# Shorter steps for the edge loop of a graph layer: 3 tiles and 32 nodes a step, the fold in four column groups

## What is computed

```
msg  = relu(x_norm[src] + edge_attr @ W_e + b_e)        # 21250 x 512
aggr = segment_sum(msg, dst, num_segments=1250)         # 1250 x 512
h    = (1 + eps) * x_norm + aggr
h    = silu(bn(h @ W1 + b1)) ; h = silu(bn(h @ W2 + b2)) ; x = x + h
x    = x + experts(layernorm(x))
```

## Time and profile before

| | |
|---|---|
| median of 3 executions | 615.01 us (614.53 to 616.93) |
| the profiled execution | 615.38 us, of which the span of the trace is 613.6 us |
| PE busy in the span | 492.7 us (80%) |
| DVE, ACT, POOL busy | 391.9, 324.5, 257.3 us |
| mean granted clock of PE | 0.91 |
| edge loop, from the first gather to the first matmul behind the loop | 30.4 to 283.9 us |
| relu of a tile (L611) | 596 ns, 167 times |

### The profile page before, as it was taken

One profiled execution on the slowest core, in us unless ns is written; L12 is line 12 of the kernel. 1 busy time (PEld: TensorE's weight loads), 2 busy tenths in 40 slices (PEclk: granted clock), 3 DMA queues, 4 the chain that ended last, 5 costly groups with the idle time before them and its releaser, 6 DMA issues.

```text
span 613.6 us, 11694 instructions
## 1 busy us (share of the span) xinstructions
PE 492.7 (80%) x4023; PEld 317.0 (52%) x4023; DVE 391.9 (64%) x961; ACT 324.5 (53%) x660; POOL 257.3 (42%) x245
## 2 busy tenths in 40 slices
PE   2469769899899989998999965702599999999990
PEld 2313223333333333343466434502599999999980
DVE  5847767667666666664689457685766767665530
ACT  3526555455555555544684057534066667566650
POOL 1077777777777777100000000000535564655341
PEclk9959899899999999998999987855599999999996
DMA  9887777777777777217079007910159999974331
GB/s 220 256 300 241 213 209 230 227 221 228 228 216 230 227 225 230 64 44 266 22 262 285 20 14 222 313 62 1 51 188 290 271 301 282 278 206 75 48 44 21
DMA packets 48944, 112.46 MB, mean 183 GB/s; under 512 B 7144, under 2 KB 7564, under 8 KB 48885
## 3 DMA queue, kind: packets, MB, share of 16 engines
q0 software_dynamic: 18992, 54.02, 32.3%
q1 hardware_dynamic: 29399, 57.16, 29.2%
q10 hardware_dynamic: 494, 0.52, 0.4%
HBM read 98.88 MB, written 12.79 MB: 182 GB/s over the span
## 4 chain that ended last, share of the span: by engine, by line
PE 63%; DVE 11%; ACT 9%; DMA 5%; issue 5%; POOL 2%; DVEq 1%; SPq 1%; POOLq 0%; ACTq 0%
PE bank L1355 22%; PE bank L1536 11%; PE bank L1325 11%; PE bank L1346 7%; ACT big L611 3%; DVE bank L977 3%; PE bank L1562 2%; PE bank L1334 2%; PE bank L1526 2%; PE bank L1517 2%; POOL pair L486 1%; DVE rows_z L1176 1%; PE bank L1399 1%; PE bank L1405 1%; DMA xs_home<-in_x 1%
## 5 line engine op out<-in xcount | busy, mean ns | idle before, releaser
L1325 PE MATMUL bank<-big,edge_home 128*64 128x256 f32 x668 | 109.4, 420 | 30.9 <-ACT big L611 30.5
L611 ACT ACTIVATE big<-bank 128x512 f32<-128x512 f32 x167 | 99.5, 596 | 65.1 <-DVE bank L977 63.5
L496 POOL DMA_INDIRECT big<-token_rows,idx x32 | 37.4, 1170 | 222.4 <-DVE idx L1234 215.0
L486 POOL DMA_INDIRECT pair<-node_rows,edge_home x97 | 96.3, 993 | 29.6 <-issue 28.7
L1355 PE MATMUL bank<-big,pair 128*128 128x156 f16 (+2 forms) x1056 | 106.5, 260 | 1.1 <-DVE big L1033 0.9
L1355 PEld LDWEIGHTS bank<-big,pair 128*128 128x128 f16 x1056 | 80.9, 97 | 24.6 <-issue 1.4
L486 POOL DMA_INDIRECT big<-node_rows,edge_home x70 | 70.5, 1006 | 49.3 <-issue 48.3
L1325 PEld LDWEIGHTS bank<-big,edge_home 128*64 128x64 f32 x668 | 35.4, 140 | 88.3 <-issue 58.4
L1346 PE MATMUL bank<-edge_home 64*128 64x512 f16 x501 | 73.6, 401 | 3.9 <-DVE edge_home L950 3.9
L505 POOL DMA_INDIRECT out<-rows_z,idx x32 | 51.5, 1610 | 43.8 <-issue 24.6
L977 DVE TENSOR_TENSOR bank<-pair,bank 128x512 f32<-128x512 f32 x97 | 64.1, 687 | 6.2 <-PE bank L1346 6.1
(11 more groups left out here) (222 smaller groups left out, 778.0 us busy)
## 6 DMA issues: line engine op xcount, KB each, us to landing
raw<-in_L_ffn_w SPq DMA_DIRECT2D x12, 1024.0 KB, 8.3
edge_home<-in_L_ffn_w SPq DMA_DIRECT2D x6, 1024.0 KB, 8.6
pair<-in_L_ffn_w SPq DMA_DIRECT2D x6, 1024.0 KB, 9.9
edge_home<-in_edge_attr SPq DMA_DIRECT2D x19, 320.0 KB, 4.0
xs_home<-in_x SPq DMA_DIRECT2D x10, 448.0 KB
xs_home<-in_L_ffn_w SPq DMA_DIRECT2D x4, 1024.0 KB, 8.8
aggT<-in_L_ffn_w SPq DMA_DIRECT2D x4, 1024.0 KB, 11.1
node_rows<-xs_home SPq DMA_DIRECT2D x5, 448.0 KB
```

The costliest lines, as they stand in the source:

```text
L486: pool.indirect_dma_start(row(t), None, node_rows, bass.IndirectOffsetOnAxis(src_i[:, t:t + 1], 0)).then_inc(row_in[t % RR], 16)
L496: pool.indirect_dma_start(xg[e % XR][:, a, :], None, token_rows, bass.IndirectOffsetOnAxis(idx[:, e, a:a + 1], 0)).then_inc(xg_in[e % XR], 16)
L611: act.activation(msg[:, t % MR, :], bank[t % PB][0:Q, :], ACT.Relu, scale=1.0 / E_SCALE).then_inc(msg_ready, 1)
L1325: done = pe.matmul(bank[6 + b][a * WIN:(a + 1) * WIN, 0:HB], onehot[b][:, j, :], msg[:, t % MR, a * HB:(a + 1) * HB], start=(j == 0), stop ...
```

## The change

A step becomes 3 tiles (56 steps) and its window 32 nodes. With `FG` = 128 / `WIN` the fold uses four column groups of 32, each with 128 message columns: eight matmuls a tile. A step's sum is 128 by 128, and its turn is one transpose. The copy and the turn of the last step's sum move ahead, behind the first tile of the next step, and the accumulation comes behind its third. The chunks become complete at steps 13, 24 and 36; their products lie in eight of the ten steps that follow, behind the second tile, and are copied out one step later (`ZLAG` = 1). The last product is in step 46 of 56. SP waits until four gathered rows are used before it loads W1. The split of W_e moves into the normalisation of the rows.

```diff
-J = 5
+J = 3
-    WIN = 64
+    WIN = 32
-    SLOPE, OFFSET = 33.0, 14.0
-    ZSTART = (9, 17, 25)
-    ZOFF = (0, 1, 2, 3, 4, 5, 6, 7)
-    ZLAG = 0
+    SLOPE, OFFSET = 21.5, 14.0
+    ZSTART = (13, 24, 36)
+    ZOFF = (0, 1, 2, 4, 5, 6, 8, 9)
+    ZLAG = 1
-        edge_home = sb("edge_home", [128, 5220], F32)
+        edge_home = sb("edge_home", [128, 4900], F32)
 # SP
+            sp.wait_ge(row_used, 1 + 4)
             for k in range(HK):
                 sp.dma_start(W1_32[:, k, :], W1_t[:, k, :]).then_inc(w1_in, 16)
 # ACT, normalisation
+                if g == 2:
+                    act.wait_ge(params_in, 48)
+                    act.activation(We16[:, 0, :], We32[:], ACT.Copy, scale=E_SCALE).then_inc(We_halves, 1)
 # ACT, step
-                    if j == 1 and i >= 1:
+                    if j == min(0, last) and i >= 1:
                         sum_copy(w, i - 1)
-                    if j == min(3, last) and i - ZLAG in part_at:
+                    if j == min(1, last) and i - ZLAG in part_at:
                         part_copy(w, part_at[i - ZLAG])
 # DVE, ahead of the loop (moved from right before it)
+            dve.wait_ge(We_halves, 1)
+            dve.scalar_tensor_tensor(out=We16[:, 1, :], in0=We32[:], scalar=E_SCALE, in1=We16[:, 0, :],
+                                     op0=ALU.mult, op1=ALU.subtract).then_inc(We_halves, 1)
 # DVE, step
-                    if j == min(3, last) and i >= 1:
+                    if j == min(2, last) and i >= 1:
                         accumulate(w, i - 1)
 # PE, step
-                    if j == 1 and i >= 1:
+                    if j == 0 and i >= 1:
                         turn_sum(w, i - 1)
-                    if j == min(2, last) and i in part_at:
+                    if j == min(1, last) and i in part_at:
                         part_product(w, part_at[i])
```

More of the change, by code:

```diff
@@ L628, in _ @@
             act.wait_ge(vec_ps, 3)
-            act.wait_ge(params_in, 48)
-            act.activation(We16[:, 0, :], We32[:], ACT.Copy, scale=E_SCALE).then_inc(We_halves, 1)
             act.sem_inc(msg_ready, 1)
@@ L992, in step @@
                     accumulate(w, i)
-            dve.wait_ge(We_halves, 1)
-            dve.scalar_tensor_tensor(out=We16[:, 1, :], in0=We32[:], scalar=E_SCALE, in1=We16[:, 0, :],
-                                     op0=ALU.mult, op1=ALU.subtract).then_inc(We_halves, 1)
             run_steps(dve, n_pass, SB, step)
```

## The result

The changed kernel takes 596.57 us (median of 4, 595.17 to 598.31) against 614.77 us for the kernel before (4 executions). The ratio is 0.971, with an interval of 0.967 to 0.975: some 18 us faster. The forecast of 587.5 us was 9 us too low; the time lies inside the forecast's range and short of rival (2), 598.

The account below looks back on a forecast made before the run. POOL's gathers set a floor; the arithmetic lagged behind them. Last add 26.9 us earlier plus tail 2.4 gave 29.3 off 615.38, 586.1 us; with 1.5 of lag left, 587.5. Range 582.5 to 601.

Parts of the forecast that it names:

- rival (2): Edge loop: hand-offs of 0.2 us, or a lower PE clock, keep 56 steps off the floor: 598 us; chance 0.14.
- The floor: POOL's gathers in the edge loop, 1.30 us a tile, 217.4 us in all; no arithmetic change moves the last one.
- The prices on PE: PE in the edge loop: fold 0.36 us, turn 0.26, pair of edge terms 0.75, product 1.40.
- Rival (4): PE's fold gains nothing: four column groups run one after the other, or issue binds; 605 us, chance 0.14.
- The tail: Last add to first matmul behind the loop: 3.8 us in place of 6.25, a gain of 2.4.
- W1's place: Ahead of tile 42: W1 loaded behind the first gathers, so the first should land after about 3.8 us instead of 6.9.
- What fills the lag: Adds fall 27 us behind gathers over the loop: PE's work, with product-copy waits of 0.59 us in 24 steps, 14 us.
- The 6 us that the arithmetic should win on POOL: From tile 42 on: 156 us of arithmetic against 162 us of gathers for 125 tiles.
- The lag ahead of the sum: At tile 42 a tile's add should stand 9 to 12 us behind its gather.
- the ring: Turn, accumulation, next add, relu, fold and pair through the engines: 3.2 us a step on average, under 3.9 of gathers.
- Rival (3): Slower: the ring carries product, statistics and both pair halves in each step, 4.7 us a step; 629 us, chance 0.04.
- rival (1): Floor is reached and falls as W1 leaves the first gathers' queues: 582.5 us; chance 0.67 together with the forecast.

Follow-up runs that it names:

- the later splits: DVE's second half of each split (W1, chunks, attributes) put later than ACT's first half, against the changed kernel: 589.67 us, ratio 0.960.
- The best kernel here: Changed kernel with DVE's second halves of the splits later and each product behind the third tile of its step: 585.42 us, ratio 0.955.
- the old steps without waits: Kernel before, 5 tiles a step, two column groups: product behind second tile, copy behind fifth, statistics a step later, DVE's low halves later: 589.92 us, ratio 0.961.

## Why the prediction came out as it did

**The floor** was right. POOL's gathers end within 4 us of where they did, and in each kernel whose lag came down to 5 to 7 us the time stayed between 585 and 590 us. That no change of the arithmetic moves the last gather was too strong: with two column groups, the later turn and the copy in its own step it starts at 255.8, 258.6 and 282.9, since the ring of rows was full.

**The prices on PE** were right at the full clock, each within 0.01 us: fold 0.36, turn 0.26, pair 0.75. The hand-off of 0.1, which was assumed, was about right too: the six from the last add to the conversion behind the loop take 0.03 to 0.15 us. Rival (4) fell by the rows and by the run with two groups.

**The tail** was right: 3.74 us, with 3.8 forecast. In the old steps it stays 6.25 us even with the waits of the loop taken out (250.77 to a first matmul at 257.02), because the last product still lies in the last step there; ACT's copy of it waits as in the earlier trace rows, and the last sum's copy stands behind it:

```profile
254.51 0.47 ACT L601 ACTIVATE raw<-bank,colA 128x250 f32<-128x250 f32 x1 [2.14 <-PE bank L1357]
```

By these rows the 2.5 us belong mostly to the last product's earlier place, as forecast. Whether steps of 5 with that place would have them too was not run.

**W1's place** was right in that it costs nothing; the wait gains nothing either. **The split of W_e** may cost something after all: the first gather starts at 30.0 to 30.4 us in the three kernels that have it right ahead of the loop, and at 30.6 to 32.5 in the eleven that have it in the normalisation. No run moves it alone.

**What fills the lag** was wrong. I read it as PE's own work with 14 us of waits on top, and so made the cheaper fold the main term of the change, 37 us. The kernel before with only the product's waits taken out has the same lag at tile 42 (9.8 and 9.3) and 10.0 at the end where it had 30.8. So all the growth behind tile 42 in the kernel before, 21 us, was those waits, and the old folds kept up with the gathers. The term had been worked out from one place, 0.59 us, times 24. The waits of the whole stretch from 95 to 240 us stood in the trace of before, and I didn't read them:

```profile
ACT xs_home L601 <- PE bank L1355: 29.5, 13, 3.1
...
DVE st L966 <- ACT xs_home L601: 18.8, 13, 2.1
```

DVE's waits there are 1.45 us each, over twice those of the step that I took.

**The 6 us that the arithmetic should win on POOL** from tile 42 on were mis-sized, and this is the term of the forecast that missed. Measured: lag of 14.3 at tile 42 (12 at most), 159.2 us of arithmetic (156), 157.7 us of gathers (162, since they came 1.27 apart and not 1.30). 14.3 + 159.2 - 157.7 is the lag of 15.8. So the reserve was -1.5. The faster gathers change the lag and not the time, since the arithmetic set the end.

The lag ahead of the sum came as forecast: at tile 41 it is 11.9. The 14.3 have the first chunk's split in them, which the forecast counts in its 156, and so the sum is short by more than the 3.2 us of the difference. From one step's first add to the next step's, the 24 steps with a product took 95.7 us (93 by the forecast's prices), the two left with a split 10.7 (10.6), and the other 15 took 52.0, 3.47 each, where the ring was put at 3.2 (48). What one step delays can turn up in a later one, so these sums don't name the cause. The run with the later second halves does: it is for the most part the splits. A chunk's split left PE idle for 2.6 to 3.0 us, where DVE's 2.1 were counted, and the lower clock behind it lengthens the next steps, which was not in the sum at all; nor were DVE's waits for the attributes' halves, 2.0 us between 95 and 240. With all second halves a step later the lag is 6.6 at tile 42 and 7.0 at the end.

That the time lies inside the range is in part luck: its upper end was there for rivals (2) and (4), and neither reason came true.

**Rival (2)** had the place and nearly the time, but not the reason. The loop did stay off the floor; the clock did fall, further than it says, to 0.67 in the first stretch. There, and at the end of the loop, a clock of 1.00 brings no time. Between 95 and 240 us the low clock stands behind the splits and goes with them, so there it is a part of their price, of unknown size. And with its 56 steps and the later splits the loop does reach the floor, so it isn't the hand-offs that hold it off.

**Rival (3)** had the mechanism of the two largest losses. The ring is there, by these two prices: the turn one tile later costs 37 us, the copy in its own step 46. The change holds both apart, so it had no say.

**How the parts add up.** Taken out of the changed kernel one by one, fold (24), turn (37) and copy (46) sum to 107 us, of a gain of 18. They aren't terms of a sum. A step of three tiles creates the tight ring in which each of them is needed; the old step had room, and in it the copy alone does what the whole change does.

**What stays open.** Why the gathers ran 4 us faster after the change wasn't sought. W1 is not the reason that rival (1) makes of it: with W1 ahead of the gathers again they take 212.9 us from the first start to the last end. The best kernel here (585.4) and the old steps without waits (589.9) are 4.5 us apart and their intervals touch; the tail, where the first matmul behind the loop comes at 254.18 and 257.02 us, gives 2.8 of it.

## What to carry to other kernels

Find the floor first, then ask of every lag whether it is work or waits, and sum the waits over the whole stretch in the view that groups them; one step is no sample. Such a sum is a candidate and no price: take the wait out in a run, since here one that grew from 10 to 31 us cost nothing. On an engine that takes its work in the order written, an instruction that waits for another engine's half delays every tile queued behind it, and to put it one step later cost nothing here; try this before the arithmetic is made cheaper. A busy share of 94% on one engine doesn't make it the bound while the lag behind the pacemaker stays constant.

## What was not expected of the hardware

Matmuls in different column groups with 128 f32 columns start on average at most 0.036 us apart, 16 in 0.58 us with their weight loads. Two short f32 matmuls a tile, whose result nobody reads, lift the granted clock of a stretch from 0.67 to 1.00, and of another from 0.61 to 1.00, and no time is gained, since PE waits for others there. Behind a wait of 3 us for a chunk's split the same product took 2.68 us in place of 1.48. The longest gathers of a later stretch fell from 1800 to 1539 ns with POOL's code unchanged.
